# Rotated projections of a three-stage decoder layer: the cosine product moves to VectorE, the low part to GpSimd, and four PSUM banks take turns in all three projection phases

## The chip, the cores and the metric

The kernel runs on one core of a Trainium2 chip. The metric is the device time of one execution in microseconds (us): the median of three runs.

## The reference

Four sequences (batches) of 512 rows of width 512 go through three blocks, each with a residual. Below, LN is layer normalization without weights, RMS the root-mean-square one with weights.

```python
x = x + attn(LN(x))                    # 16 heads of 32, causal, no rotation
x = x + xattn(LN(x), ctx, pos, pos)    # 32 heads of 16, keys and values from ctx (width 256)
x = x + ffn(LN(x))                     # h = RMS(LN(x)); q, k, v = h @ w + b; 16 heads of 32, causal; then experts

# rotation of q and k in xattn: pairs of neighbouring elements
out = stack([x1 * cos - x2 * sin, x1 * sin + x2 * cos])
# rotation of q and k in ffn: halves of a head
q * cos + rot(q) * sin
```

## The kernel before

The program is a sequence of phases that are closed off from each other by a barrier of all engines: for each of the kinds `first`, `cross` and `rotary` a projection phase (line 244) and an attention core, and at the end the experts. The change lies in the projection phase. It makes q, k and v of all four batches and stores them in memory for the core. All products are made in three passes of high and low parts (`hi_lo_passes`), so each tensor that TensorE reads exists as a rounded high part and a remainder.

For each batch TensorE works through a ring of items: q, k and v of feature tile m = 0 to 3, in the order q0, k0, v0, q1, ... (in the last batch v2 and v3 come after k3). An item fills one PSUM bank with a 128x512 tile: q always takes 12 matmuls, k and v take 12 in `rotary` and 6 in `cross`, where the context is 256 wide. The ring has four banks (4 to 7), but only two (6 and 7) in `cross`, because the context's transposes sit in banks 4 and 5 (line 309). TensorE starts an item when the item N_RING places before it has been freed (`freed`, line 312). For q and k that is ScalarE's copy `straight`.

In what follows a **step** i is one q or k: i = 8 * batch + 2m, plus 1 for k, so there are 32. The rotation of step i goes over four engines:

- ScalarE copies the bank to `straight` (L538 with bias in `rotary`, L540 in `cross`), scaled for q.
- GpSimd multiplies `straight` by cosine into `turned` (L722).
- VectorE exchanges partitions of `straight` into `swapped` (L694, `stream_shuffle`), and GpSimd multiplies that by sine (L724).
- VectorE adds both (L645, `rotate`), ScalarE rounds the sum to its high part (L475, `high`), VectorE subtracts to get the low part (L650, `low`), and SyncE stores both (L384).

All these tiles have two slots. Every engine works in its own fixed order. VectorE does in step i: exchange i, low part i-2, sum i-1. ScalarE does: copy i, high part i-2. GpSimd does: cosine i, sine i, where cosine i waits for low part i-2, which frees its slot.

Beside that, the next batch's input is prepared in parts at fixed places (line 295). `NORM_AT = (0, 2, 4)` names the steps of a batch behind which VectorE does the parts of `norm`: statistics, centring (with sums of squares in `rotary`), and the second scaling in `rotary`. `ROOT_AT` names those behind which ScalarE takes the roots. `TURN_AT = 6` is the step behind which TensorE transposes the new input into banks 0 to 3 (`turn_in`, with the context behind it), ScalarE writes its high parts (`hT_high`) and VectorE its low parts (`hT_low`). TensorE's first q of the next batch waits for all of them.

In `rotary`, centring writes `h1`, which SyncE also stores to memory. There is one `h1` tile, so the centring of batch b+1 waits for the store of batch b (line 590), and that store stands in SyncE's queue behind all stores of batch b-1 (line 359 ff.). SyncE's queue also loads three stacks for the core in the middle of the last two batches (`STACK_AT`), ten transfers each in `cross` and five in `rotary`.

## Time and profile before

| | |
|---|---|
| median of 3 runs | 2296.25 us (2291.01 to 2301.59) |
| profiled execution: its own time | 2297.42 us |
| profiled execution: its span | 2295.6 us |
| mean granted clock of TensorE in it | 0.938 |
| TensorE busy | 2069.8 us (90%) |
| VectorE busy | 1237.3 us (54%) |
| ScalarE busy | 881.1 us (38%) |
| GpSimd busy | 708.3 us (31%) |
| first `straight` copy to last low part, `cross` | 472.9 to 615.4 us of the span |
| the same, `rotary` | 1081.9 to 1235.7 us |

The profile has one execution. Its time outside of the span is 1.8 us. The two projection phases that the change touches take together about 310 us of it. A page's row of a group gives busy time, count and mean; a row of a timeline gives the start in us, the duration in us, engine, line and operation, and in brackets the idle time before it with what ended it.

### The profile page before, as it was taken

What the parts mean: (1) busy time and instruction counts of PE and PEld (TensorE: products, weight loads), DVE (VectorE), ACT (ScalarE), POOL (GpSimd) and SP (SyncE); (2) the same over time, 40 slices, a digit from 0 to 9 for tenths busy, and PEclk for the clock granted to TensorE, in tenths of its full rate; (3) what the DMA queues carried; (4) which work ended last, traced back from release to release, by engine and by line L of the source; (5) the groups of instructions that cost most, each with busy time, mean ns of one, the idle gap of its engine ahead of it and who ended that gap; (6) DMA issues with size and microseconds to landing.
All of it is one profiled execution on the core that took longest, in us unless ns stands there. A gap on an engine that the chain in (4) does not pass through costs nothing. (4 is left out here: it accounts for less than half of the span.)

```text
span 2295.6 us, 31417 instructions
## 1 busy us (share of the span) xinstructions
PE 2069.8 (90%) x10679; PEld 1384.3 (60%) x10679; DVE 1237.3 (54%) x2679; ACT 881.1 (38%) x1662; POOL 708.3 (31%) x610
## 2 busy tenths in 40 slices
PE   6998999887689999996987999979999988999998
PEld 5775666565433434334776666657788877565664
DVE  5446656377689788875976656534313142222221
ACT  3335444343368676773334544433212210111111
POOL 0004555346513232322554654511000000233332
PEclk9997999989789999998997999889999998999999
DMA  5557666345654545443457665453012043433332
GB/s 188 172 192 174 140 136 136 113 163 217 254 127 100 132 116 152 103 124 117 179 192 227 151 152 128 102 200 110 30 63 74 1 172 117 142 60 59 63 65 36
DMA packets 149937, 297.14 MB, mean 129 GB/s; under 512 B 23762, under 2 KB 42324, under 8 KB 148756
## 3 DMA queue, kind: packets, MB, share of 16 engines
q1 hardware_dynamic: 113972, 243.73, 36.6%
q10 hardware_dynamic: 27072, 32.77, 5.3%
q0 software_dynamic: 8736, 18.62, 4.3%
q8 instruction: 88, 1.44, 0.3%
q14 instruction: 69, 0.57, 0.1%
HBM read 181.55 MB, written 102.50 MB: 124 GB/s over the span
## 5 line engine op out<-in xcount | busy, mean ns | idle before, releaser
L1157 ACT ACTIVATE cross_c_prob<-bank 128x512 f32<-128x512 f32 x512 | 271.3, 598 | 124.4 <-PE bank L996 123.4
L1194 DVE TENSOR_REDUCE cross_c_row_max<-bank 128x2 f32<-128x1024 f32 x256 | 300.0, 1212 | 34.8 <-PE bank L965 29.0
L996 PE MATMUL bank<-stack 56*128 56x512 f32 (+4 forms) x768 | 238.7, 437 | 34.1 <-DMA stack<-first_c_max_rows 11.4
L1577 PE MATMUL bank<-moe_hT,moe_w 128*128 128x512 f32 x1056 | 261.5, 405 | 2.2 <-DVE moe_hT L1819 2.2
L965 PE MATMUL bank<-stack 48*128 48x512 f32 (+4 forms) x768 | 218.1, 465 | 36.1 <-PEq L70 19.5
L1577 PEld LDWEIGHTS bank<-moe_hT,moe_w 128*128 128x128 f32 x1056 | 206.5, 197 | 47.3 <-DVE moe_hT L1819 2.6
L996 PEld LDWEIGHTS bank<-stack 56*128 56x128 f32 (+1 forms) x768 | 122.6, 198 | 164.8 <-ACT cross_c_prob L1157 70.3
L1665 PE MATMUL bank<-moe_w_e,moe_hT_e 128*128 x624 | 195.0, 466 | 1.6 <-DMA moe_w_e<-in_experts_packed 1.2
L965 PEld LDWEIGHTS bank<-stack 48*128 48x128 f32 (+1 forms) x768 | 107.4, 206 | 123.6 <-DVE cross_c_row_max L1194 51.7
L1190 DVE CUSTOM_DVE_ANT_0 first_c_masked<-bank,later 128x128 f32<-128x128 f32 (+3 forms) x256 | 115.8, 486 | 88.5 <-PE bank L965 87.6
L1190 DVE CUSTOM_DVE_ANT_0 rotary_c_masked<-bank,later 128x128 f32<-128x128 f32 (+3 forms) x256 | 116.0, 486 | 85.8 <-PE bank L965 84.9
L1157 ACT ACTIVATE rotary_c_prob<-bank 128x512 f32<-128x512 f32 (+3 forms) x256 | 105.5, 437 | 134.2 <-PE bank L999 132.7
L1157 ACT ACTIVATE first_c_prob<-bank 128x512 f32<-128x512 f32 (+3 forms) x256 | 105.2, 437 | 134.3 <-PE bank L999 133.0
L1665 PEld LDWEIGHTS bank<-moe_w_e,moe_hT_e 128*128 128x128 f32 x624 | 116.5, 192 | 63.5 <-issue 5.5
L1950 DVE TENSOR_TENSOR moe_prod<-moe_prod,bank 128x512 f32<-128x512 f32 x44 | 30.2, 687 | 205.7 <-PE bank L1577 205.7
L1037 PE MATMUL bank<-cross_c_prob,cross_c_v 128*32 128x512 f32 x1024 | 138.9, 615 | 0.6 <-DVE cross_c_flipped L1205 0.6
L1533 POOL DMA_INDIRECT out_x<-moe_res,moe_token x39 | 61.9, 1587 | 228.1 <-ACT moe_res L1774 228.1
L1588 PE MATMUL bank<-moe_w,moe_inner 128*128 128x512 f32 x528 | 127.9, 391 | 0.0
L999 PE MATMUL bank<-earlier_r,ident_r 128*128 128x128 f32 x512 | 125.7, 246 | 0.0
L1516 POOL TENSOR_TENSOR moe_res<-moe_res,moe_x_tile 128x512 f32<-128x512 f32 x16 | 23.3, 1455 | 323.1 <-DMA moe_x_tile<-x 323.1
L1588 PEld LDWEIGHTS bank<-moe_w,moe_inner 128*128 128x128 f32 x528 | 99.2, 188 | 21.5
L999 PEld LDWEIGHTS bank<-earlier_r,ident_r 128*128 128x128 f32 x512 | 105.5, 206 | 7.2
(344 smaller groups left out, 3967.8 us busy)
## 6 DMA issues: line engine op xcount, KB each, us to landing
moe_w_e<-in_experts_packed SPq DMA_DIRECT2D x8, 2176.0 KB, 9.0
qk_parts<-first_p_parts SPq DMA_DIRECT2D x32, 512.0 KB, 2.7
stack<-qk_parts SPq DMA_DIRECT2D x64, 256.0 KB, 6.9
qk_parts<-cross_p_parts SPq DMA_DIRECT2D x32, 512.0 KB, 2.7
stack<-qk_parts SPq DMA_DIRECT2D x256, 64.0 KB, 2.4
qk_parts<-rotary_p_parts SPq DMA_DIRECT2D x32, 512.0 KB, 2.7
moe_raw<-in_shared_packed SPq DMA_DIRECT2D x11, 768.0 KB, 11.5
stack<-qk_parts SPq DMA_DIRECT2D x16, 512.0 KB, 5.1
```

The source lines that it names most:

```text
L965: last = nc.tensor.matmul(bank[:, 0 : width_q(m)], q_stack[slot][r : r + PRODUCT_ROWS, at, m * P : (m + 1) * P], k_stack[slot][r : r + PRO ...
L996: last = nc.tensor.matmul(bank[:, 0 : S - q0], k_stack[slot][r : r + ALL_ROWS, at, m * P : (m + 1) * P], q_stack[slot][r : r + ALL_ROWS, a ...
L999: last = nc.tensor.matmul(bank[:, 0:P], c.ident_r[:], c.earlier_r[:], start=False, stop=True)
L1037: last = nc.tensor.matmul(psum[bank_o][32 * j : 32 * j + 32, q0:S], val, probability(g, m, j), start=m == 0, stop=m == TT - 1)
L1157: nc.scalar.activation(probability(g, step // HEADS_AT_ONCE, step % HEADS_AT_ONCE), psum[bank_at["score", n]][:, 0 : S - q0], ACT.Exp).the ...
L1190: nc.vector.tensor_tensor_reduce(out=masked[:, n % 2, 0 : width_q(m)], in0=bank[:, 0 : width_q(m)], in1=c.later[:, S - width_q(m) : S], sc ...
L1194: nc.vector.tensor_reduce(row_max[:, g % 2, m, j - 1 : j + 1], c.banks[:, first : first + WIDE, :], AX_X, ALU.max).then_inc(s.max_done, 1)
L1533: pool.indirect_dma_start(a.out, bass.IndirectOffsetOnAxis(ap=token[:, t : t + 1], axis=0), y[:, t % 2, :], None, bounds_check=B * S - 1, ...
L1577: last = nc.tensor.matmul(psum[bank][:], weights(pa, f, k), hT[p % 2][:, pb, k, :], start=m == 0, stop=m == len(steps) - 1)
L1588: last = nc.tensor.matmul(psum[SD[t]][:], inner[:, n % 2, pa, t * P : (t + 1) * P], w_d(pb, f), start=f == 0 and m == 0, stop=f == KF - 1 ...
L1665: last = nc.tensor.matmul(psum[1 + 2 * (t % 2) + half][:, 0:FE], hT_e[:, t % 2, k, :], rhs, start=k == 0, stop=k == KD - 1)
L1950: nc.vector.tensor_tensor(prod[:], prod[:], psum[SU][:], ALU.mult).then_inc(s.s_inner, 1)
```

## The change

`first` keeps its order; the rest holds for `cross` and `rotary`.

- VectorE makes the cosine product from the bank itself (`times_cos`, in `rotary` with the bias in the same instruction), in front of the exchange. The bank is now freed by that (`cos_made`) and no longer by ScalarE's copy. `turned` gets three slots.
- The low part goes from VectorE to GpSimd, behind the sine product of the following step; only the very last one stays on VectorE. ScalarE's high part moves one step forward: copy i is now followed by high part i-1 instead of i-2.
- The scale of q goes into the weights (`weights_high`, `weights_low`), so `straight` is an unscaled copy.
- The context is transposed into banks 0 and 1, behind step 5 (`CONTEXT_AT`), when the input's banks have been read; the ring has four banks in `cross` too. In batch 0 that happens behind q0.
- Norm parts move from behind steps 0, 2 and 4 to behind 0, 1 and 3, the roots from 2 and 4 to 1 and 3, the transposes from 6 to 4.

The diff, cut to its core:

```diff
+    TURNED_SLOTS = 3
-        NORM_AT, ROOT_AT, TURN_AT = (0, 2, 4), (2, 4), 6
+        NORM_AT, ROOT_AT, TURN_AT = ((0, 1, 3), (1, 3), 4) if rope else ((0, 2, 4), (2, 4), 6)
+        CONTEXT_AT = TURN_AT + 1
-        ring_banks = (6, 7) if cross else (4, 5, 6, 7)
+        ring_banks = (4, 5, 6, 7)
-            name = {...}.get(what, "straight_made" if rope else "parts_lo")
+            name = {...}.get(what, "cos_made" if rope else "parts_lo")
...
# TensorE
+                    def turn_context(bi):
+                        pe.wait_ge(s.ctx_loaded, 16 * (bi + 1))
+                        pe.wait_ge(s.hT_lo, t.n_in * bi + t.n_kv)
+                        for k in range(t.n_kv):
+                            for m in range(TT):
+                                last = nc.tensor.transpose(psum[k][:, m * P : (m + 1) * P], ctx_t[:, m, k * P : (k + 1) * P], c.ident[:])
+                        last.then_inc(s.transposed, 1)
...
+                        if cross and (bi, what, m) == (0, "k", 0):
+                            turn_context(0)
+                        if m == 0 and what in "qk":
+                            ready = t.n_in * bi + (KD if what == "q" else t.n_in)
+                            pe.wait_ge(s.hT_hi, ready)
+                            pe.wait_ge(s.hT_lo, ready)
...
+                        if cross and what in "qk" and 2 * m + (what == "k") == CONTEXT_AT and bi + 1 < BODY:
+                            turn_context(bi + 1)
...
# ScalarE
-                    hT_high(act, 0)
+                    hT_high(act, 0, range(KD))
                     weights_high(1)
+                    if cross:
+                        hT_high(act, 0, range(KD, t.n_in))
                     weights_high(2)
...
-                                act.wait_ge(s.cos_made, i - 1)
-                                nc.scalar.activation(straight[:, i % 2], bank[:], ACT.Copy, scale=scale).then_inc(s.straight_made, 1)
-                            if i >= 2:
-                                high(i - 2)
+                                nc.scalar.activation(straight[:, i % 2], bank[:], ACT.Copy).then_inc(s.straight_made, 1)
+                            if i >= 1:
+                                high(i - 1)
...
# VectorE
+                    def times_cos(i, what, m, bank):
+                        if i >= TURNED_SLOTS:
+                            dve.wait_ge(s.parts_hi, i - TURNED_SLOTS + 1)
+                            dve.wait_ge(s.parts_lo, i - TURNED_SLOTS + 1)
+                        dst, table = turned[:, i % TURNED_SLOTS], cos_t[:, i // n_qk if cross else 0]
+                        if rotary:
+                            nc.vector.scalar_tensor_tensor(dst, bank[:], bias_of(what, m), table, ALU.add, ALU.mult).then_inc(s.cos_made, 1)
+                        else:
+                            nc.vector.tensor_tensor(dst, bank[:], table, ALU.mult).then_inc(s.cos_made, 1)
...
                             dve.wait_ge(s.straight_made, i + 1)
+                            times_cos(i, what, m, bank)
                             nc.vector.stream_shuffle(swapped[:, i % 2], straight[:, i % 2], swap).then_inc(s.swap_made, 1)
-                            if i >= 2:
-                                low(i - 2)
                             if i >= 1:
                                 rotate(i - 1)
...
# GpSimd
-                            nc.gpsimd.tensor_tensor(turned[:, i % 2], straight[:, i % 2], cos_t[...], ALU.mult).then_inc(s.cos_made, 1)
                             pool.wait_ge(s.swap_made, i + 1)
                             nc.gpsimd.tensor_tensor(swapped[:, i % 2], swapped[:, i % 2], sin_t[...], ALU.mult).then_inc(s.sin_made, 1)
+                            if i >= 1:
+                                n = i - 1
+                                pool.wait_ge(s.parts_hi, n + 1)
+                                nc.gpsimd.tensor_tensor(parts[:, n % 2, 1], turned[:, n % TURNED_SLOTS], parts[:, n % 2, 0].bitcast(F32),
+                                                        ALU.subtract).then_inc(s.parts_lo, 1)
```

Two places show how rows move. The first is GpSimd's order in `cross`, two steps long (`axial_cos` and `axial_sin` are the tables, `parts` holds high and low part). Before:

```order
L722 TENSOR_TENSOR cross_p_turned<-cross_p_straight,axial_cos 128x512
L724 TENSOR_TENSOR cross_p_swapped<-cross_p_swapped,axial_sin 128x512
L722 TENSOR_TENSOR cross_p_turned<-cross_p_straight,axial_cos 128x512
L724 TENSOR_TENSOR cross_p_swapped<-cross_p_swapped,axial_sin 128x512
```

Now:

```order
L752 TENSOR_TENSOR cross_p_swapped<-cross_p_swapped,axial_sin 128x512
L756 TENSOR_TENSOR cross_p_parts<-cross_p_turned,cross_p_parts 128x512
L752 TENSOR_TENSOR cross_p_swapped<-cross_p_swapped,axial_sin 128x512
L756 TENSOR_TENSOR cross_p_parts<-cross_p_turned,cross_p_parts 128x512
```

The number of two-input products on GpSimd stays at two a step; the cosine product is gone and the low part of the step before stands behind the sine.

The second is VectorE's order in `rotary`, batch 0, around the scaling; `hn` is the scaled input of the next batch, `hT_lo` the low part of its transpose. Before: step 4, the scaling, step 5 and v2, with the low part of the transpose not before step 6 is done:

```order
L694 STREAM_SHUFFLE rotary_p_swapped<-rotary_p_straight 128x512
L650 TENSOR_TENSOR rotary_p_parts<-rotary_p_turned,rotary_p_parts 128x512
L645 TENSOR_TENSOR rotary_p_turned<-rotary_p_turned,rotary_p_swapped 128x512
L610 RECIPROCAL rotary_p_rstd<-rotary_p_rms 128x4
L612 TENSOR_SCALAR rotary_p_hn<-rotary_p_h1,rotary_p_rstd 128x512 x4
L694 STREAM_SHUFFLE rotary_p_swapped<-rotary_p_straight 128x512
L650 TENSOR_TENSOR rotary_p_parts<-rotary_p_turned,rotary_p_parts 128x512
L645 TENSOR_TENSOR rotary_p_turned<-rotary_p_turned,rotary_p_swapped 128x512
L683 TENSOR_TENSOR rotary_p_v<-bank,rotary_p_bv_row 128x512
```

Now, step 3, the scaling, v1, step 4 and the low part of the new input:

```order
L661 SCALAR_TENSOR_TENSOR rotary_p_turned<-bank,rotary_p_bias_raw,rotary_p_cos_t 128x512
L726 STREAM_SHUFFLE rotary_p_swapped<-rotary_p_straight 128x512
L670 TENSOR_TENSOR rotary_p_turned<-rotary_p_turned,rotary_p_swapped 128x512
L623 RECIPROCAL rotary_p_rstd<-rotary_p_rms 128x4
L625 TENSOR_SCALAR rotary_p_hn<-rotary_p_h1,rotary_p_rstd 128x512 x4
L714 TENSOR_TENSOR rotary_p_v<-bank,rotary_p_bv_row 128x512
L661 SCALAR_TENSOR_TENSOR rotary_p_turned<-bank,rotary_p_bias_q,rotary_p_cos_t 128x512
L726 STREAM_SHUFFLE rotary_p_swapped<-rotary_p_straight 128x512
L670 TENSOR_TENSOR rotary_p_turned<-rotary_p_turned,rotary_p_swapped 128x512
L466 SCALAR_TENSOR_TENSOR rotary_p_hT_lo<-bank,rotary_p_w_ln,rotary_p_hT_hi 128x512 x4
```

VectorE has three instructions a step in both; the low part's place is taken by the cosine product ahead of the exchange, and one step instead of two lies between the scaling and the low part of the transposed input.

## Rows read from the trace of the kernel before

**Rows 1.** By stretch: busy us of PE, PEld, DVE, ACT, POOL; PEclk, DMA, GB/s.

```profile
456.00:615.00 159.00, 116.16 (x480) 91.85 (x480) 114.54 (x208) 62.73 (x112) 95.70 (x64) 0.88 0.55 200
1060.00:1236.00 176.00, 146.55 (x640) 119.33 (x640) 141.97 (x275) 57.28 (x92) 93.40 (x64) 0.93 0.56 192
```

**Rows 2.** Waits in the cross phase: total us, times, longest us.

```profile
PE bank L434 <- DVE cross_p_hT_lo L457: 18.1, 4, 6.1
ACT cross_p_parts L475 <- DMA qk_parts<-cross_p_parts: 15.5, 4, 4.4
```

**Rows 3.** The same view of the rotary phase.

```profile
ACT rotary_p_straight L538 <- PE bank L434: 68.1, 24, 6.7
```

**Rows 4.** Timeline, rotary: two VectorE instructions (start us, duration us).

```profile
1126.82 0.68 DVE L683 TENSOR_TENSOR rotary_p_v<-bank,rotary_p_bv_row 128x512 f32<-128x512 f32 x1
...
1140.42 1.78 DVE L650 TENSOR_TENSOR rotary_p_parts<-rotary_p_turned,rotary_p_parts 128x512 fp32r<-128x512 f32 x1
```

**Rows 5.** Timeline of GpSimd in the same stretch.

```profile
1126.43 1.62 POOL L722 TENSOR_TENSOR rotary_p_turned<-rotary_p_straight,rotary_p_cos_t 128x512 f32<-128x512 f32 x1 [1.98 <-DVE rotary_p_parts L650]
...
1140.37 1.28 POOL L724 TENSOR_TENSOR rotary_p_swapped<-rotary_p_swapped,rotary_p_sin_t 128x512 f32<-128x512 f32 x1
```

**Rows 6.** Timeline of VectorE, last batch of the cross phase: two projections apart.

```profile
585.47 0.77 DVE L694 STREAM_SHUFFLE cross_p_swapped<-cross_p_straight 128x512 f32<-128x512 f32 x1
586.12 0.92 DVE L650 TENSOR_TENSOR cross_p_parts<-cross_p_turned,cross_p_parts 128x512 fp32r<-128x512 f32 x1
...
592.43 0.76 DVE L694 STREAM_SHUFFLE cross_p_swapped<-cross_p_straight 128x512 f32<-128x512 f32 x1
```

**Rows 7.** Timeline of ScalarE in the same stretch.

```profile
596.98 0.63 ACT L475 ACTIVATE cross_p_parts<-cross_p_turned 128x512 fp32r<-128x512 f32 x1 [2.13 <-DVE cross_p_turned L645]
597.52 0.58 ACT L540 ACTIVATE cross_p_straight<-bank 128x512 f32<-128x512 f32 x1
```

**Rows 8.** Timeline of ScalarE at the start of the cross phase.

```profile
466.78 1.10 ACT L487 ACTIVATE cross_p_w_hi<-raw 128x1024 fp32r<-128x1024 f32 x1
```

**Rows 9.** Tile swapped, cross: ns min/median/max, first and last start us.

```profile
L694 DVE STREAM_SHUFFLE cross_p_swapped<-cross_p_straight x32: 720/742/767, 473.5 to 607.2; 128x512 f32<-128x512 f32 x32
```

**Rows 10.** Tile parts, cross: the same columns.

```profile
L650 DVE TENSOR_TENSOR cross_p_parts<-cross_p_turned,cross_p_parts x32: 670/693/978, 479.8 to 614.7; 128x512 fp32r<-128x512 f32 x32
```

**Rows 11.** Tile parts, rotary: the same columns.

```profile
L650 DVE TENSOR_TENSOR rotary_p_parts<-rotary_p_turned,rotary_p_parts x32: 664/684/1798, 1091.3 to 1235.0; 128x512 fp32r<-128x512 f32 x32
```

**Rows 12.** Timeline of VectorE, rotary: first exchanges of batches 1 and 3.

```profile
1120.15 0.73 DVE L694 STREAM_SHUFFLE rotary_p_swapped<-rotary_p_straight 128x512 f32<-128x512 f32 x1
...
1201.80 0.73 DVE L694 STREAM_SHUFFLE rotary_p_swapped<-rotary_p_straight 128x512 f32<-128x512 f32 x1
```

**Rows 13.** Timeline of VectorE, rotary batch 1: norms and turned inputs of batch 2.

```profile
1121.97 2.46 DVE L576 BATCH_NORM_STATS2 rotary_p_stats<-xt 128x6 f32<-128x512 f32 x4
...
1132.72 1.91 DVE L592 TENSOR_SCALAR rotary_p_h<-xt,rotary_p_mv,rotary_p_rstd 128x512 f32<-128x512 f32 x4 [2.17 <-DMA h<-rotary_p_h]
...
1137.24 0.17 DVE L607 TENSOR_SCALAR rotary_p_ssq<-rotary_p_ssq 128x4 f32<-128x4 f32 x1
...
1142.93 3.52 DVE L612 TENSOR_SCALAR rotary_p_hn<-rotary_p_h,rotary_p_rstd 128x512 f32<-128x512 f32 x4
...
1151.76 2.71 DVE L455 SCALAR_TENSOR_TENSOR rotary_p_hT_lo<-bank,rotary_p_w_ln,rotary_p_hT_hi 128x512 fp32r<-128x512 f32 x4
```

**Rows 14.** Timeline of SyncE's queue, rotary.

```profile
1127.21 0.78 SPq L361 DMA_DIRECT2D h<-rotary_p_h  x1
```

**Rows 15.** Timeline of TensorE, rotary: the first matmul of batch 3.

```profile
1196.44 0.61 PE L434 MATMUL bank<-rotary_p_hT_hi,rotary_p_w_hi 128*128 128x512 f32 x1 [3.75 <-DVE rotary_p_hT_lo L455]
```

**Rows 16.** Timeline of ScalarE, rotary batch 3: copies of the first two projections.

```profile
1201.07 0.69 ACT L538 ACTIVATE rotary_p_straight<-bank,rotary_p_bias_q 128x512 f32<-128x512 f32 x1 [5.32 <-PE bank L434]
1203.81 0.69 ACT L538 ACTIVATE rotary_p_straight<-bank,rotary_p_bias_raw 128x512 f32<-128x512 f32 x1 [1.54 <-PE bank L434]
```

**Rows 17.** Busy time behind that idle time; 0.62 is PEclk.

```profile
1197.00:1201.00 4.00, 4.00 (x13) 3.14 (x12) 1.72 (x3) 0.00 (x0) 2.83 (x2) 0.62 0.64 224
```

More of the change, by code:

```diff
@@ L552, in _ @@
                             if i % n_qk == TURN_AT:
[L553 removed]
+                                hT_high(act, bi + 1, range(KD))
+                            if cross and i % n_qk == CONTEXT_AT:
+                                hT_high(act, bi + 1, range(KD, t.n_in))
                 @block.vector
@@ L706, in _ @@
                             if i % n_qk == TURN_AT:
-                                hT_low(dve, bi + 1)
+                                hT_low(dve, bi + 1, range(KD))
+                            if cross and i % n_qk == CONTEXT_AT:
+                                hT_low(dve, bi + 1, range(KD, t.n_in))
                 @block.gpsimd
```

63 lines of the change are left out of this document (28 added, 35 removed).

## The prediction

> **What bounds the kernel now.** I read the page first: TensorE is busy 90% of the span, but that is an average over seven phases, and the change touches two. So the next view is the busy time of these two stretches [rows 1]. In `cross`, 159 us long, TensorE works 116 us, VectorE 115 and GpSimd 96: nobody is full. In `rotary`, 176 us, TensorE has 147 and VectorE 142. The waits say who waits for whom. In `cross` TensorE stands 18.1 us in four places because the next input's low parts are late, and ScalarE waits 15.5 us for stores of `parts` to land [rows 2]. In `rotary` ScalarE waits 68.1 us for TensorE's banks [rows 3]: that phase goes at TensorE's pace.
>
> The timelines give the reason for the pace of `cross`. A VectorE subtraction with both inputs in SBUF took 1.78 us when a GpSimd product had started 0.05 us before it, and ended 0.55 us after that one [rows 4, 5]; undisturbed it takes 0.69 [rows 10]. They exclude each other. VectorE's addition with one input in a bank took 0.68 us right through a GpSimd product [rows 4, 5]. Before, each step holds two such VectorE instructions and two GpSimd products: 2 x 0.6 + 2 x 1.28 = 3.8 us where they all collide. Measured, two steps take 592.43 - 585.47 = 6.96 us, 3.48 a step [rows 6].
>
> **What the change does to a step.** It takes one of the excluded VectorE instructions away and puts a product with one input in a bank in its place. GpSimd keeps two products (2 x 1.28 [rows 5], plus 0.55 when it waits for the sum): 3.1 us. I price the cosine product at 0.68, by the addition out of a bank [rows 4]. The Trainium skill (Perfetto Trace Analysis, Optimizing Scalar/DVE Operations) gives VectorE an access overhead of about 125 ns on PSUM against 60 ns on SBUF; for 64 products that would be an estimated 4 us more. The row does not show it, 0.68 being no longer than the 0.69 of the subtraction in SBUF [rows 10], so my sum stays without it.
>
> But the change also ties a new knot. ScalarE's high part i-1 now stands in front of copy i+1, and it needs sum i-1, which VectorE makes last in step i. So the loop is: sum 0.68, signal 0.03, high part 0.54 until the next may start [rows 7], copy 0.58, signal 0.04, product 0.60, exchange 0.65 (the next instruction starts 0.65 after an exchange of 0.77 [rows 6]). That makes 3.1 us in `cross`, and 3.2 in `rotary`, whose copies take 0.69 [rows 16]. Before, high part i-2 left one step of slack there. So 3.48 becomes 3.1, but everything that VectorE does beside it now adds to the loop, less the 1.25 us in which ScalarE works. And where a v copy stands on ScalarE (`cross` only, about 0.5), it adds too.
>
> **The sum for `cross`.** Per batch: 8 x 3.1 = 24.8; statistics 3.1 (2.46 for the four [rows 13], 0.6 for the small ones) less 1.25 = 1.9; centring (1.9, plus 0.8 until high part and root are made, plus about 0.5 behind a GpSimd product) less 1.25 = 2.0; turned inputs 2.6 (four low parts behind ScalarE's four high parts); context and v2 1.7; v1 and v3 1.0. Together 34.0, three times; the first, with no sum to wait for, 33.4. The last batch has none of it: 7 x 3.1 + 2 x 0.5 = 22.7. The stack loads in SyncE's queue hold two stores up by some 3.4 us each; a wait of 4.4 is in the trace [rows 2], and ScalarE now stands in the loop while it waits: 6.8. First to last exchange: 33.4 + 68.0 + 22.7 + 6.8 = 130.9, before 607.2 - 473.5 = 133.7 [rows 9]. The start is later by 3.1: the context's copies and the third weight split (1.1 on ScalarE [rows 8]) now stand between q0 and its copy, and the product is ahead of the exchange. The end is earlier by 2.3: the last low part came 8.1 us behind the last exchange [rows 9, 10]; now exchange 0.74, sine 1.3, a low part in front 1.3, sum, high and low 2.0, waits 0.5, which is 5.8. Sum: -2.8 + 3.1 - 2.3 = **-2.0 us**.
>
> **The sum for `rotary`.** One projection is 2.74 us of TensorE [rows 16], twelve a batch 32.8, so a batch can't take less than 35 with its transposes. Before, two batches took 1201.80 - 1120.15 = 81.65 us [rows 12]. Now TensorE transposes behind q2 (step 4) and needs the scaling behind step 3. It gets there early and loses its lead: at best it is three items ahead. I walk from the end of that scaling: last transposes 0.5; k2, v2, q3, k3, v3, q0 6 x 2.74 = 16.4; copy 0.7; step 0 1.95; statistics 3.1; step 1 1.95. Then centring waits for the `h1` store. That store was issued 0.9 us behind low part 7 and landed 5.5 us later (1127.21 [rows 14] to 1132.72 [rows 13], a wait of 2.17); now low part 7 is GpSimd's, behind the sine of step 0, and ends 4.3 us after the copy, so `h1` lands at 10.8, and VectorE, ready at 7.8, stands 3.0 us. Centring and squares 4.7 (1132.72 to 1137.41 [rows 13]), v0 0.7, step 2 1.95, step 3 with the loop 3.25, root 0.8, scaling 2.7 (between 1.9 free and 3.52 beside GpSimd [rows 13]). From the copy on that is 24.9; a batch takes 17.6 + 24.9 = 42.5. Two: 85.0, which is +3.4. In batch 0 TensorE stands about 6 us for the scaling, half of which the vanished wait at the batch's end (3.75 in one case [rows 15]) gives back: +3.2. In the last batch the eleven items behind q0 give 30.1 us from its first exchange to the end, against 1235.7 - 1201.8 = 33.9 [rows 11, 12]: -3.7. Then the clock: behind 3.75 us of idle time [rows 15] the granted clock was 0.62 (between the levels of 1.2 and 2.4 GHz) [rows 17], and q0 took 1201.07 - 1196.44 = 4.6 us instead of 2.74 [rows 15, 16], 1.9 lost. TensorE will now stand some 4 to 6 us at three transposes; I count two of three: +3.8. Sum: **+6.7 us**.
>
> Nothing else moves: the scale in the weights costs nothing, as the same copy takes it along, and its cover is the same wait for the inputs. The profiled execution's own time is 2297.4 us, 1.2 above the median of the runs. 2297.4 - 2.0 + 6.7 = 2302.1, less 1.2: **2301 us**. A measurement of this kernel can tell about 0.5% (11.5 us) from no change, so the forecast is: no difference.
>
> **Rivals.**
>
> *Faster: the side work hides.* My terms beside the loop (9.2 us a batch in `cross`) add fully. VectorE's own busy time is only 115/4 = 28.6 us a batch [rows 1]; if four banks let it run through without gaps, three batches save 34.0 - 28.6 = 5.4 each (16), and if the stores also keep up, 6.8. With TensorE never waiting at the transposes `rotary` ends at its pace, some 5 us before today instead of 6.7 after (12). 2301 - 16 - 7 - 12 = 2266 at the far end, half way 2283. For it: 18.1 us of waits at the batch's end vanish [rows 2]. Against it: the order on ScalarE is fixed. Chance 0.2.
>
> *Slower: TensorE loses its lead and its clock.* Besides the transposes it must wait for the bank of v0, which VectorE frees only behind centring and squares; that is 3 us idle in front of q2. If each of those six gaps is followed by a slow projection, 1.9 each, `rotary` gains 7.6 us on top, and each wait for `h1` may be 3 us longer where the store lands late: 2301 + 7.6 + 6 = 2315. It decides from gaps of about 3.75 us on [rows 15], the shortest after which these rows show a slow projection. Chance 0.2.
>
> *Slower: stores.* `parts` has two slots, and high part i waits for the store of i-2. I leave about 1 us of slack a step. If stores take 1.5 us more, each second step pays: 32 x 0.75 = 24, so 2325. The 15.5 us of such waits [rows 2] speak for it, the steadier order against it. Chance 0.07.
>
> *The change doesn't free the engines.* If the product out of the bank excludes GpSimd too, up to 1.1 us (1.78 - 0.68) is lost on it, on half of 64 products 35 us: 2336. Rows 4 and 5 speak against it. Chance 0.03.
>
> **Numbers.** Forecast 0.5, faster 0.2, slower 0.2 + 0.07 + 0.03. Faster by over 0.5% (below 2284.8) takes 0.18 of the faster case and 0.02 of the forecast's own spread: 0.2. Slower (above 2307.7) takes 0.17, 0.07 and 0.03 of the three and 0.02 of the forecast: 0.29. Within: 0.51. The range leaves out the far ends on both sides: 2280 to 2318.
>
> **What would show it.** In the profile after: exchanges in `cross` 3.1 to 3.6 us apart in the last batch, against 3.48; no VectorE subtraction of 1.8 us but sums of up to 1.9; the products out of the bank at 0.68 beside GpSimd; no wait of TensorE for low parts at the batch's end, but in `rotary` one of 3 to 6 us in front of the transposes; centring waiting about 3 us for `h1`; first exchanges of `rotary` batches 1 and 3 near 1121 and 1210 (moved with the end of `cross`). Wrong: exchanges under 3.0 us apart, or `rotary` batches under 38 us, would make it faster; products of 1.2 us and more, or waits of ScalarE for stores above 30 us in a phase, slower.

## The result, and the profile after

| | before | changed |
|---|---|---|
| median of the runs beside the prediction (4 each) | 2297.61 us (2291.01 to 2301.59) | 2319.79 us (2318.73 to 2322.35) |
| ratio, 95% interval | | 1.0101 (1.0075 to 1.0127) |
| timed again on one chip (23 and 6 runs) | 2301.03 us | 2322.79 us, 1.0099 (1.0080 to 1.0118) |
| profiled execution: own time, span | 2297.42, 2295.6 us | 2320.35, 2318.5 us |

Slower by 1.0%, the interval clear of no change: forecast 2301 (2280 to 2318), measured 2320. Below, "first to last exchange" is the pace of a phase; "front" is from the phase's first statistics instruction to its first exchange, "tail" from the last exchange's start to the start of the last low part. They are read from the tile views.

| us | before | changed | forecast change | measured change |
|---|---|---|---|---|
| cross: front | 19.8 | 21.7 | +3.1 | +1.9 |
| cross: first to last exchange | 133.7 | 139.0 | -2.8 | +5.3 |
| cross: tail | 7.5 | 4.9 | -2.3 | -2.6 |
| rotary: front, exchanges, tail together | 175.8 | 187.4 | +6.7 | +11.6 |
| all other stretches | 1958.8 | 1965.5 | 0 | +6.7 |

The exchanges of both phases, changed kernel, tile view (ns min/median/max, first and last start in us), against 473.5 to 607.2 before [rows 9]:

```profile
L726 DVE STREAM_SHUFFLE cross_p_swapped<-cross_p_straight x32: 715/730/754, 480.3 to 619.3; 128x512 f32<-128x512 f32 x32
...
L726 DVE STREAM_SHUFFLE rotary_p_swapped<-rotary_p_straight x32: 715/732/754, 1092.2 to 1249.8; 128x512 f32<-128x512 f32 x32
```

Busy time by stretch, changed kernel (columns as in [rows 1]; the stretches are chosen alike):

```profile
461.00:624.00 163.00, 111.70 (x480) 89.93 (x480) 102.10 (x208) 60.69 (x111) 90.47 (x63) 0.86 0.54 194
1070.00:1255.00 185.00, 150.61 (x640) 123.30 (x640) 130.58 (x273) 56.71 (x92) 91.56 (x63) 0.91 0.52 178
```

VectorE did lose work: 114.5 us busy in cross became 102.1, 142.0 in rotary 130.6 [rows 1]. Yet both phases got longer, and every engine stands more. The waits say for what. Changed kernel, cross, then rotary (total us, times, longest us):

```profile
ACT cross_p_parts L486 <- DVE cross_p_turned L670: 66.5, 27, 5.1
POOL cross_p_swapped L752 <- DVE cross_p_swapped L726: 65.2, 32, 21.9
DVE cross_p_turned L663 <- ACT cross_p_straight L551: 38.1, 22, 4.7
...
PE bank L407 <- DVE cross_p_hT_lo L468: 23.1, 3, 7.7
ACT cross_p_parts L486 <- DMA qk_parts<-cross_p_parts: 21.0, 5, 5.4
...
ACT rotary_p_parts L486 <- DVE rotary_p_turned L670: 98.0, 30, 10.0
...
DVE rotary_p_turned L661 <- ACT rotary_p_straight L549: 33.2, 19, 5.1
...
PE bank L443 <- DVE rotary_p_v L714: 8.5, 3, 3.5
```

ScalarE waits for VectorE's sum (L670), and VectorE for ScalarE's copy (L551): each for the other, in turn. In rotary ScalarE waited 68.1 us for TensorE before [rows 3]; now it waits 98.0 for the sum. The phase no longer goes at TensorE's pace.

### The profile page after: what moved, and what is told of

Read it like the earlier page. It is cut to its first block, busy times and chain, and to the rows that moved or that the text cites. A ratio compares the mean times of both kernels' runs of the same rounds, so it can differ in the third digit from the quotient of the medians.

```text
span 2318.5 us, 31374 instructions
## 1 busy us (share of the span) xinstructions
PE 2073.8 (89%) x10679; PEld 1387.6 (60%) x10679; DVE 1218.2 (53%) x2681; ACT 878.8 (38%) x1662; POOL 700.8 (30%) x608
## 4 chain that ended last, share of the span: by engine, by line
PE 52%; DVE 12%; DMA 5%; issue 5%; ACT 2%; POOL 1%; SPq 1%; ACTq 0%; POOLq 0%; DVEq 0%
PE bank L1610 10%; PE bank L1698 8%; PE bank L1070 4%; PE bank L1621 4%; PE bank L1717 4%; PE bank L443 4%; PE bank L998 4%; PE bank L1029 4%; DVE cross_c_row_max L1227 4%; PE bank L1087 3%; DMA stack<-rotary_c_max_rows 1%; DMA stack<-cross_c_max_rows 1%; DMA normed<-xt 1%; PE bank L1038 1%; PE bank L1032 1%
## 5 line engine op out<-in xcount | busy, mean ns | idle before, releaser
L1070 PE MATMUL bank<-cross_c_prob,cross_c_v 128*32 128x512 f32 x1024 | 139.0, 615 | 0.6 <-DVE cross_c_flipped L1238 0.6
L1032 PE MATMUL bank<-earlier_r,ident_r 128*128 128x128 f32 x512 | 125.9, 246 | 0.0
```

What stands on the lines that cost most here:

```text
L1032: last = nc.tensor.matmul(bank[:, 0:P], c.ident_r[:], c.earlier_r[:], start=False, stop=True)
L1070: last = nc.tensor.matmul(psum[bank_o][32 * j : 32 * j + 32, q0:S], val, probability(g, m, j), start=m == 0, stop=m == TT - 1)
```

## The loop and the context, read from the trace

The step itself is what I had forecast. Changed kernel, VectorE in the last steps of cross batch 1 (start us, duration us, then the idle time before and its releaser):

```profile
538.93 0.73 DVE L726 STREAM_SHUFFLE cross_p_swapped<-cross_p_straight 128x512 f32<-128x512 f32 x1
539.55 0.68 DVE L670 TENSOR_TENSOR cross_p_turned<-cross_p_turned,cross_p_swapped 128x512 f32<-128x512 f32 x1
541.97 1.29 DVE L468 TENSOR_TENSOR cross_p_hT_lo<-bank,cross_p_hT_hi 128x512 fp32r<-128x512 f32 x2 [1.74 <-ACT cross_p_hT_hi L459]
545.67 0.69 DVE L663 TENSOR_TENSOR cross_p_turned<-bank,axial_cos 128x512 f32<-128x512 f32 x1 [2.42 <-ACT cross_p_straight L551]
...
546.29 0.74 DVE L726 STREAM_SHUFFLE cross_p_swapped<-cross_p_straight 128x512 f32<-128x512 f32 x1
546.92 0.68 DVE L670 TENSOR_TENSOR cross_p_turned<-cross_p_turned,cross_p_swapped 128x512 f32<-128x512 f32 x1
548.78 0.69 DVE L663 TENSOR_TENSOR cross_p_turned<-bank,axial_cos 128x512 f32<-128x512 f32 x1 [1.19 <-ACT cross_p_straight L551]
...
549.39 0.74 DVE L726 STREAM_SHUFFLE cross_p_swapped<-cross_p_straight 128x512 f32<-128x512 f32 x1
```

From exchange 546.29 to 549.39 is a plain step: 3.10 us. The sum ends its part, ScalarE makes high part and copy, and VectorE stands 1.19 us before the product. The step before it, 538.93 to 546.29, is the one with the context: 7.36 us, 4.26 more than a plain one, where I had allowed 1.7. TensorE and ScalarE show why (same columns):

```profile
537.36 1.94 PE L407 MATMUL bank<-ident,cross_p_ctx_t 128*128 128x128 f32 x8 [7.70 <-DVE cross_p_hT_lo L468]
```

```profile
540.82 0.63 ACT L486 ACTIVATE cross_p_parts<-cross_p_turned 128x512 fp32r<-128x512 f32 x1 [2.98 <-DMA qk_parts<-cross_p_parts]
541.35 1.06 ACT L459 ACTIVATE cross_p_hT_hi<-bank 128x512 fp32r<-128x512 f32 x2
542.31 0.60 ACT L533 ACTIVATE cross_p_v<-bank 128x512 f32<-128x512 f32 x1
545.04 0.60 ACT L551 ACTIVATE cross_p_straight<-bank 128x512 f32<-128x512 f32 x1 [2.14 <-PE bank L443]
```

The context goes into the inputs' banks, so TensorE can't start it before VectorE has made the inputs' low parts out of them. It stands 7.70 us, holds back every projection queued behind, and ScalarE then waits 2.14 us for the next bank. Three times that, 23.1 us. Before, TensorE waited for low parts too, 18.1 us in front of the first items of the four batches [rows 2]; but of those only 3.3 us are left when the places of the side work move and nothing else (below, "The kernel before, new places in cross alone"). The 23.1 us come with turning the context apart.

## Experiments

Ratios are against the kernel before on the same chip; the lengths of phases are from each run's profile.

**The kernel before, again.** No edit.

> The kernel before, unchanged, profiled once more. The changed kernel's profile is 22.9 us longer than the one of before, of which some 16 lie in the two projection phases and 4.2 + 3.9 in code that the change does not touch (the first core phase and what follows the second rotary core). If these two are spread between executions, this run shows stretches of untouched code that differ by 2 to 4 us from the first profile of before, while cross (133.7 from first to last exchange) and rotary (145.8) stay within 1 us. If the change costs them too (by what it leaves behind in queues), both stay as they were within 1 us.

Span 2304.2 us, 8.6 over the first profile. Cross 134.0, rotary 145.7: both within 0.3 us. From the last low part of the first projection to the cross statistics 296.5 instead of 291.2; from the experts' first VectorE product (L1950) to the end 753.5 instead of 748.0. So the untouched code is what varies; the projections can be compared to a few tenths here. Over all pairs of profiles with the same code in a phase their lengths agree within 1.4 us. Over all 18 profiles the untouched stretches add up to between 1957 and 1973 us.

**High part i-2 in the changed kernel.**

```diff
-                            if i >= 1:
-                                high(i - 1)
+                            if i >= 2:
+                                high(i - 2)
...
-                                n = i - 1
+                            for n in ([i - 2] if i >= 2 else []) + ([i - 1] if i == BODY * n_qk - 1 else []):
```

> High part i-2 instead of i-1 behind copy i, low part on GpSimd likewise; everything else as changed. Theory A (the loop sum, high part, copy, product, exchange through ScalarE makes all side work additive): the loop is cut, the last cross batch goes at GpSimd's pace (about 3.0 a step instead of 3.1), steps with statistics and centring get shorter by up to 1.2 us each; cross first to last exchange 139.0 becomes 131 to 134, rotary 157.6 becomes 150 to 153, the ends grow by 1 to 2 us each; whole kernel 8 to 13 us faster than the changed one. Theory B (the early places of scaling and transposes cost TensorE its lead, the loop is beside the point): both stretches move by less than 3 us, whole kernel within 4 us of the changed one.

2354.05 us, ratio 1.0209 (1.0179 to 1.0240); cross 147.5, rotary 178.5. Neither theory had this. Plain steps are 4.41 us apart, and the row says why (VectorE, last cross batch):

```profile
607.85 0.69 DVE L663 TENSOR_TENSOR cross_p_turned<-bank,axial_cos 128x512 f32<-128x512 f32 x1 [2.51 <-POOL cross_p_parts L755]
```

The product now waits for GpSimd's low part. With three slots I had opened one loop and closed another, so this run says nothing on the first.

**The old places for the side work.** One line; centring, roots and transposes as before, in both phases.

```diff
-        NORM_AT, ROOT_AT, TURN_AT = ((0, 1, 3), (1, 3), 4) if rope else ((0, 2, 4), (2, 4), 6)
+        NORM_AT, ROOT_AT, TURN_AT = (0, 2, 4), (2, 4), 6
```

> Centring, roots and turned inputs back at the steps where they stood before (0, 2, 4; 2, 4; 6), the context one step behind; everything else as changed. Theory B: rotary's TensorE waits for low parts and scaling get shorter by 2 to 3 us in three batches and its clock stays up, rotary first to last exchange 157.6 becomes 147 to 150; the wait for the store of h1 (2.93 each, twice) vanishes, since centring of the second batch's part stands a step later; whole kernel 6 to 10 us faster. Theory A: the sum of VectorE's work in the loop is the same, only its place differs; rotary gains at most the 5.9 us of the two waits for h1, cross nothing.

2307.75 us, ratio 1.0007 (0.9989 to 1.0026). Rotary 157.6 became 146.9, cross 139.0 became 136.6. TensorE's clock in rotary, first to last exchange (columns as in [rows 1]), changed kernel and this run:

```profile
1092.20:1249.80 157.60, 139.17 (x598) 113.98 (x597) 109.05 (x234) 45.13 (x79) 88.26 (x61) 0.95 0.50 174
```

```profile
1093.30:1240.20 146.90, 135.56 (x594) 110.26 (x593) 111.33 (x235) 45.06 (x79) 88.14 (x61) 0.97 0.54 187
```

TensorE is busy 3.6 us less for the same matmuls (some 1 us of it are four matmuls that this trace lacks), at a higher clock, and idle for 11.3 us instead of 18.4. Theory B is borne out in place, and in rotary all but in size (146.9 against 147 to 150). The whole was not as expected: the ratios of this kernel and the changed one lie 0.9% apart, some 22 us, where the two phases give 13.

**The store of `h1` earlier.** In SyncE's queue the store of the next batch's `h1` stands ahead of that of k2.

> The store of h1 of the next batch goes into SyncE's queue ahead of that of k2 instead of behind the batch's last store. The wait of VectorE for it (2.93, twice, in rotary) should vanish. Theory A: VectorE is in the loop, so the whole 5.9 us come off rotary's 157.6. Theory B: TensorE's stands set the pace of rotary, and centring is only one link before them: 3 to 6 us. If neither (the wait is covered by others): less than 2 us. In cross nothing changes.

2323.48 us, ratio 1.0081 (1.0055 to 1.0107). The wait is gone, and rotary is 153.5 instead of 157.6: 4.1 us, as Theory B had it. The whole time doesn't show it; this run's untouched stretches are the longest of all, 1973 us. The phase answers, the total does not.

**Transposes at 6, centring early.**

```diff
-        NORM_AT, ROOT_AT, TURN_AT = ((0, 1, 3), (1, 3), 4) if rope else ((0, 2, 4), (2, 4), 6)
+        NORM_AT, ROOT_AT, TURN_AT = ((0, 1, 3), (1, 3), 6) if rope else ((0, 2, 4), (2, 4), 6)
```

> Centring and roots stay at the changed kernel's early steps (0, 1, 3; 1, 3), only the transposes go back from step 4 to 6. Theory B1 (it is the place of the transposes that costs rotary its 10.7 us, since at step 4 TensorE reaches them before the scaling is done, and all twelve items until the next ones start late): rotary, first to last exchange, 157.6 becomes 146 to 149; cross near the 136.6 of the run with all old places. Theory B2 (it is the early centring, with VectorE's stand for the store of h1): rotary stays at 154 to 158, since that stand remains.

2323.02 us, ratio 1.0101 (1.0075 to 1.0127). Rotary 153.6: between the two theories. The transposes' place gives 4.0 of the 10.7 us, the place of centring, scaling and roots the other 6.7, and VectorE still stands 6.1 us for the store of `h1`, as it does in the changed kernel (6.0). In cross, 146.3, both missed: ScalarE waits up to 6.3 us for a store in the step before the transposes of the inputs. Why that store is later here was not tried.

**The kernel before with the new places.**

```diff
-        NORM_AT, ROOT_AT, TURN_AT = (0, 2, 4), (2, 4), 6
+        NORM_AT, ROOT_AT, TURN_AT = ((0, 1, 3), (1, 3), 4) if rope else ((0, 2, 4), (2, 4), 6)
```

> The kernel before (cosine product on GpSimd, low part on VectorE, high part i-2, context turned with the inputs, two banks in cross) with the new places alone (0, 1, 3; 1, 3; 4). If the places cost rotary its time whatever the step loop is, rotary becomes 155 to 160 instead of 145.7, as in the changed kernel. If the places only cost because VectorE stands in the new loop, it stays within 3 us of 145.7. Cross: the transposes for inputs and context at step 4 meet low parts that are done at once; 130 to 137 against 133.8.

2304.18 us, ratio 1.0015 (0.9999 to 1.0030). Rotary 160.9, a little above my 155 to 160: TensorE waits there 10.2 us for the bank of v0 and 9.6 us for the scaled input, and centring 11.5 us for the store of `h1`. **Cross 122.2**: 11.5 us shorter than before and below my range. That one line is worth more in cross than I had forecast for the whole change, and rotary takes it back.

**Cross new with the context at 6, rotary old.**

> Rotary with the old places, cross with the new ones (4), but the context's transposes at step 6 instead of 5. If the 7.35 us from exchange 5 to exchange 6 in cross come from TensorE waiting for the inputs' low parts before it may reuse their banks (7.7 us), that step falls to about 4.5 and cross from 139.0 to 131 to 134 in three batches; rotary is 146 to 148 as in the run with all old places. Whole kernel: 3 to 6 us under the run with all old places. If the context costs the same wherever it stands, cross stays at 137 to 140.

2301.73 us, ratio 1.0006 (0.9992 to 1.0021). Cross 133.4, rotary 145.5. The step from exchange 5 to 6 of batch 1 fell from 7.36 to 4.36 us (531.76 to 536.12), as expected. But the context now stands in the next step, which rose from 3.10 to 4.29, so the move gives 1.8 us in this batch. Cross came where it should, rotary 0.5 us below. The whole missed: level with before, its ratio the same as that of the run with all old places, not 3 to 6 us under it.

**High part i-2, exchange ahead of the product, old places.**

> The first run with high part i-2 closed another loop that I had not seen: the product for i waits for GpSimd's low part i-3, which stands behind sine i-1, and exchange and sine i stand behind the product (0.69 + 0.74 + 1.29 + 1.29 + signals = 4.4 a step, 4.41 measured). Here the exchange goes ahead of the product, so that loop opens; places as before. Theory A (the loop through ScalarE makes side work additive): steps beside statistics and centring up to 1.2 us shorter than in the run with all old places, plain steps 3.0 to 3.1; cross 136.6 becomes 130 to 133, rotary 146.9 becomes 141 to 145. Theory B: plain steps as fast, but both stretches within 2 us of 136.6 and 146.9, because TensorE's waits at the transposes set the batch.

2326.05 us, ratio 1.0102 (1.0077 to 1.0127); cross 139.1, rotary 157.4. Both theories missed. Plain steps did fall, in the last cross batch to 2.8 to 3.2 us (exchanges at 592.72, 595.51, 598.48, 601.54, 604.72), but another wait took over, here in its cross phase:

```profile
ACT cross_p_parts L486 <- DMA qk_parts<-cross_p_parts: 42.2, 14, 6.9
```

A low part made by GpSimd a step later leaves a step later for memory, and `parts` has two slots.

**Low part back on VectorE, high part i-2 and i-1.** GpSimd keeps the sine product alone; the product out of the bank stays on VectorE. `cross` has the new places, `rotary` the old ones. The two kernels differ only in this, and in the lines that go with it at the end of the last batch:

```diff
-                            if i >= 2:
-                                high(i - 2)
+                            if i >= 1:
+                                high(i - 1)
```

> Cosine product stays on VectorE, the low part goes back to VectorE (i-2), high part i-2; GpSimd has the sine product alone. Cross with the new places and the context at step 5, rotary with the old places. VectorE then has 0.69 + 0.65 + 0.67 + 0.68 = 2.7 a step, excluded pairs 0.67 + 0.68 + 1.28 = 2.6. Theory C (GpSimd's late low part delays the store, and ScalarE waits for the slot: 42.2 us in 14 waits in the run with high part i-2 and the exchange first): those waits fall to under 15 us in cross, plain steps to 2.7 to 2.9, cross 139.0 to 115 to 125, rotary to 138 to 145, whole kernel 10 to 20 us faster than before. If the low part on GpSimd is not what costs, cross stays above 132.

> The same with high part i-1 in front of copy i+1, as the change has it: the only difference to the run before it. Theory A (sum, high part, copy, product, exchange form a loop through ScalarE, 3.1 us, beside which side work adds fully): plain steps 3.1, cross 8 to 15 us longer than in the run before it, rotary 3 to 8 longer. Without such a loop: within 2 us of it in both.

2328.47 us, ratio 1.0119 (1.0086 to 1.0153), and 2386.97 us, ratio 1.0371 (1.0340 to 1.0403). Cross 140.7 and 172.0, rotary 161.8 and 184.1. Theory C missed: the waits for stores are down to 8.2 us, yet plain steps take 3.52. The sums of the first of the two (ns min/median/max):

```profile
L663 DVE TENSOR_TENSOR cross_p_turned<-bank,axial_cos x32: 675/678/692, 479.8 to 620.5; 128x512 f32<-128x512 f32 x32
L670 DVE TENSOR_TENSOR cross_p_turned<-cross_p_turned,cross_p_swapped x32: 677/1768/1785, 485.2 to 624.0; 128x512 f32<-128x512 f32 x32
```

The sum, both inputs in SBUF, meets the sine product in most steps and takes 1.77 us instead of 0.68; the product out of the bank is never stretched. Of the second kernel Theory A had the loop right and the size far too small (8 to 15 us in cross and 3 to 8 in rotary; measured 31.3 and 22.3): with high part i-1 the slow sum lies in the loop. From its start to that of the high part are 1.79 us, then to copy, product, exchange, low part and next sum 0.54, 0.61, 0.62, 0.61 and 0.59, together 4.76; plain exchanges are 4.79 apart (635.29, 640.08). One `high` moved by a step costs 31 us in cross. The plain step alone, 1.27 us longer, would make 39 in 31 steps, so what costs here is the step and not side work that adds. And high part i-2 alone doesn't let a loop catch up: in the first kernel batch 1 takes 38.7 us against 28.2 for eight plain steps, 10.5 us of side work. VectorE works there without a gap in a plain step.

**The kernel before, new places in cross alone.**

```diff
-        NORM_AT, ROOT_AT, TURN_AT = (0, 2, 4), (2, 4), 6
+        NORM_AT, ROOT_AT, TURN_AT = ((0, 1, 3), (1, 3), 4) if cross else ((0, 2, 4), (2, 4), 6)
```

> The kernel before with the new places in cross alone; rotary keeps the old ones. The two profiles at hand give the parts: cross 122.2 with the new places and the old step loop, rotary 145.8 with the old places. If the two phases are independent, cross is 122 to 124, rotary 145 to 147, and the whole kernel 10 to 12 us faster than before (ratio 0.995). If the gain in cross is given back behind it (the core that follows waits for something else), cross is as short but the whole within 4 us of before.

**2288.23 us, ratio 0.9946 (0.9927 to 0.9964)**: a little faster than before, and so than the changed kernel. Cross 121.8, rotary 144.9. TensorE's waits for low parts in cross, 18.1 us before [rows 2], are down to the first one:

```profile
PE bank L434 <- DVE cross_p_hT_lo L457: 3.3, 1, 3.3
```

How the old loop takes the side work, VectorE, cross batch 1:

```profile
511.54 0.72 DVE L694 STREAM_SHUFFLE cross_p_swapped<-cross_p_straight 128x512 f32<-128x512 f32 x1
...
513.57 3.65 DVE L592 TENSOR_SCALAR cross_p_hn<-xt,cross_p_mv,cross_p_rstd 128x512 f32<-128x512 f32 x4
...
517.15 0.73 DVE L694 STREAM_SHUFFLE cross_p_swapped<-cross_p_straight 128x512 f32<-128x512 f32 x1
...
519.18 0.75 DVE L694 STREAM_SHUFFLE cross_p_swapped<-cross_p_straight 128x512 f32<-128x512 f32 x1
...
522.38 1.33 DVE L645 TENSOR_TENSOR cross_p_turned<-cross_p_turned,cross_p_swapped 128x512 f32<-128x512 f32 x1 [1.63 <-POOL cross_p_swapped L724]
...
523.84 0.74 DVE L694 STREAM_SHUFFLE cross_p_swapped<-cross_p_straight 128x512 f32<-128x512 f32 x1
```

A step with centring, 5.61 us, is followed by one of 2.03, together 7.64. Steps of this loop go in such pairs without side work too, in the last batch 2.31 and 4.65, together 6.96; so centring costs 0.7 us here. In the changed kernel its step takes 5.88, 2.8 more than a plain one, and no step is under 3.09. By batch: batch 1 takes 33.4 us here against 27.4 for eight steps at the last batch's mean of 3.43, which leaves 6.0 for the side work; in the changed kernel 36.9 against 24.8, which leaves 12.1. The shorter plain step saves 2.6 us a batch, and the side work beside it costs 6.1 more.

**The same, and transposes of rotary at 5.**

> As the run before it, and in rotary the transposes one step earlier, at 5 instead of 6, centring unmoved. Theory B (TensorE reaches the transposes before the scaling is done, when they stand early): scaling is done behind step 4, TensorE is two to three items ahead, so it stands there 2 to 4 us but no longer 3.1 us for low parts at the batch's end: rotary 144 to 152. Step 4 gave 160.9, step 6 gave 145.8; a value near 160 would mean that any step before 6 is too early.

2305.10 us, ratio 1.0008 (0.9992 to 1.0025). Rotary 155.5, above my 144 to 152: one step too early already costs 10 us; of the steps 4, 5 and 6 only 6 holds. Which wait makes it 155.5 was not looked at.

**Banks and context apart, old loop.** The changed kernel with the cosine product back on GpSimd, the low part on VectorE and high part i-2, the bank freed by ScalarE's copy and two slots of `turned`; the scale stays in the weights; cross new, rotary old; context at step 5, then 6.

> The change without its step loop: four banks in cross and the context turned apart in the inputs' banks at step 5, but the cosine product on GpSimd, the low part on VectorE, high part i-2 as before; cross with the new places, rotary with the old. If the step loop is what costs cross its 17 us, cross is 118 to 126 (two banks more can only let TensorE run ahead). If the context turned apart is what costs (TensorE waits 7.7 us for low parts at each of three), cross is 134 to 139. In between, both.

> The same with the context's transposes at step 6 instead of 5. In the changed step loop that move gave 5.6 us (139.0 to 133.4). If the wait of TensorE for the inputs' low parts costs the same beside the old loop, cross is 4 to 7 us under that of the run with step 5; if the old loop hides it, within 2 us.

2297.07 us, ratio 0.9980 (0.9966 to 0.9995), and 2294.35 us, ratio 0.9974 (0.9959 to 0.9990). Cross 125.9 and 123.7: the first at the upper end of my 118 to 126, where the step loop is what costs cross its 17 us. TensorE stands 19.0 us for the low parts there, nearly as long as in the changed kernel (23.1), and the phase is 3.7 us over the one without that stand. Moving the context gives 2.2 us here, not the 5.6 of the changed loop. Rotary, 145.5, is as before (145.8), with the scale in the weights.

**The changed kernel and the best one, again.** No edit against those two.

> The changed kernel itself, unchanged, timed in more rounds. If the 1.010 was right: 1.008 to 1.012 against the kernel before on the same chip. If before's first four runs were low by the spread of untouched code (its later medians were 2300.9 to 2304.6, in place of 2297.6): about 1.007, some 17 us. The stretches of the two projections stay within 1 us of the first profile (139.0 and 157.6), the untouched first core and the part behind the second core vary by up to 6 us.

> The kernel before with the new places in cross alone, timed again beside the changed kernel on one chip. The first measurement gave 0.9946, with the interval 0.9927 to 0.9964: again 0.993 to 0.996, and 25 to 32 us under the changed kernel. Its cross 121 to 123, rotary 144 to 147.

2322.79 us, ratio 1.0099 (1.0080 to 1.0118); cross 139.3, rotary 157.0. And 2290.71 us, ratio 0.9952 (0.9933 to 0.9970); cross 122.7, rotary 146.1. The 1.010 was right, and the two kernels are 32 us apart on one chip.

**The ledger that closes.** First to last exchange, us, adding one part of the change at a time:

| | cross | rotary |
|---|---|---|
| before | 133.7 | 145.8 |
| + new places | 122.2 (-11.5) | 160.9 (+15.1) |
| + four banks, context apart at step 5 | 125.9 (+3.7) | (not run with new places) |
| + step loop: the whole change | 139.0 (+13.1) | 157.6 (-3.3) |

The row of the banks holds the scale in the weights as well, and was run with cross alone at the new places; cross with and without rotary's new places is 122.2 and 121.8. In rotary the change of banks touches nothing, and the loop is worth -3.3 at the new places, +1.1 at the old ones (146.9 against 145.8; the run with the context at 6 has the same code in rotary and 145.5, so this is no more than the spread). The loop's +13.1 in cross is by batch (the run with the context at 5, "banks5", against the changed kernel, first exchange to first exchange): 30.4 and 35.8, 36.1 and 36.9, 35.1 and 37.3, last 24.3 and 29.1. The last one has no side work. In both kernels ScalarE waits for stores there, twice each; banks5, then the changed kernel:

```profile
ACT cross_p_parts L486 <- DMA qk_parts<-cross_p_parts: 7.3, 2, 3.7
```

```profile
ACT cross_p_parts L486 <- DMA qk_parts<-cross_p_parts: 10.4, 2, 5.4
```

Only in the changed loop do steps show it, 6.60 and 6.48 us long; in banks5 none of that batch is over 4.65.

No run takes high part i-1 alone out of the changed loop: the two that tried closed another wait. So the +13.1 is shown for the loop as a whole, and its share of lag and of order is not.

## Why the prediction was wrong

The forecast for the profiled execution was 2302.1 us; it took 2320.4, 18.2 more: 6.6 in cross, 4.9 in rotary, 6.7 elsewhere. The step that failed most is the term "context and v2" of the sum for cross; in rotary it is the last batch, where I had put a wait for a store at nothing.

- **The step of 3.1 us: right.** 3.10 in cross, 3.25 in rotary, and 3.57 with a v copy. The product out of the bank took 0.69 in cross (678/691/695 ns; 0.75 in rotary, with the bias) and didn't mind GpSimd: the one at 532.84 ran 0.69 us inside a GpSimd low part (532.26, 1.26 us). That rival (0.03) fell. The Trainium skill (Perfetto Trace Analysis, Optimizing Scalar/DVE Operations) would have had it dearer than one in SBUF. The trace has, with both inputs in SBUF, the last low part at 692 ns and the sums at a median of 675; so of the 65 ns between the page's two figures at most 16 show.
- **The sum of cross per batch: 34.0 forecast, 36.9 measured** (batch 1). By terms: statistics 1.75 for 1.9; centring, with the copy of v0, 2.8 for 2.0; turned inputs 2.4 for 2.6; v1 and v3 0.97 for 1.0; context and v2 **4.26 for 1.7**. Over the three batches that term is 12.5 us for 5.1, 7.4 of the 8.1 by which first to last exchange missed. The failed step is "context and v2 1.7": I priced copies and low parts, and not that TensorE must wait for the banks of the inputs before the context's transposes, up to 7.7 us in each of three batches. The run with the context at 6 bears it out: those waits for low parts fall from 23.1 to 9.1 us and cross by 5.6.
- **Last batch of cross: right**, 29.1 for 29.5. **Front and tail**: +1.9 for +3.1, -2.6 for -2.3.
- **Rotary: mechanism right, one term missing.** Centring waited 2.93 us for `h1` (forecast 3.0), and TensorE 3.38 for v0's bank (3 in the slower rival); these rows of the changed kernel:

```profile
1144.14 1.92 DVE L605 TENSOR_SCALAR rotary_p_h<-xt,rotary_p_mv,rotary_p_rstd 128x512 f32<-128x512 f32 x4 [2.93 <-DMA h<-rotary_p_h]
```

```profile
1149.50 0.50 PE L443 MATMUL bank<-rotary_p_hT_hi,rotary_p_w_hi 128*128 128x512 f32 x1 [3.38 <-DVE rotary_p_v L714]
```

  The batches are 44.25 and 44.4 us for 42.5: the two took 88.7, where 81.65 [rows 12] + 3.4 + 3.8 for the clock makes 88.9. Batch 0 took 41.75 against 37.3, +4.5 for +3.2, and the front, for which I had no change, took 0.8 more. In front of the transposes TensorE stood 2.10 and 0.68 us in batch 1, not the 4 to 6 that I had counted the clock by; the clock fell behind the stand for v0's bank as well. So of the 88.7 the walk is borne out, and that the clock's 3.8 fits is partly luck. The first exchanges of batches 1 and 3 came at 1133.96 and 1222.62, both some 13 us later than my 1121 and 1210, so the lengths between them agree. The term that failed is the last batch, forecast at 3.7 us less than before; from its first exchange to the start of the last low part it took 32.5 us against 33.2, 0.7 less. The row that I had no term for:

```profile
1231.62 0.63 ACT L486 ACTIVATE rotary_p_parts<-rotary_p_turned 128x512 fp32r<-128x512 f32 x1 [6.46 <-DMA qk_parts<-rotary_p_parts]
```

  One step takes 7.67 us (1225.87 to 1233.54), 4.4 more than a plain one, because ScalarE stands in the loop until a store has landed. Before, the same batch had such a wait of 1.0 us. I had counted these waits in cross (6.8) and not here. My point of decision for the clock, gaps of 3.75 us and more, was also too high (last section).
- **"Nothing else moves": open.** 6.7 of the profile's 22.9 us lie in untouched code, well inside its spread of 16. But the medians of 23 and 6 runs on one chip are 21.8 us apart, and the two phases explain about 16. The other 5 to 6 were not traced to a place; they stay open.
- **The rivals.** The nearest number is that of the slower one on TensorE's lead (2315, chance 0.2). Its wait for v0's bank came, and a lower clock behind it (last section), but not its price: batches 1 and 2 of rotary took what the forecast had, not 7.6 us more. Its number is near because cross and the last batch of rotary added what it didn't have; that is luck. The faster rival said that the side work hides; in the old loop with the new places half of it does, in the new one it doesn't.
- **What the sum didn't ask.** I set the new loop's plain step (3.1) against the old one's (3.48) and let the side work add to the new, without asking what the old loop does with side work at better places. With the new places alone the old loop keeps its mean plain step of 3.43 us, of which GpSimd works 2.9 (20.3 us in seven steps), and takes a batch's side work for 6.0 us more, where the new loop pays 12.1. Of cross before, 11.5 us lay in the places. So the change mended the wrong limit.

## What to carry to other kernels

Split a change into its one-line parts and run each alone: here the moved places were worth -11.5 us in one phase and +15.1 in the other, and kept where they help they beat both kernels (0.9946). A faster plain step is no gain if it takes the slack out of a loop: compare whole batches with their side work. In the changed loop the side work of batch 1 costs 12.1 us, in the old one at the same places 6.0. A lag of two steps is not enough for that: the loop with the low part back on VectorE has it, and adds 10.5 us in batch 1. And where a buffer is used twice in turn, price the engine's stand for its release, with all that is queued behind it.

## What the runs showed of the hardware

- An instruction of VectorE with both inputs in SBUF next to a GpSimd product: 1.77 us (median of 32 sums) instead of 0.68, where the order made them meet in most steps. GpSimd pays as well: its sine product is 1.63 us in the changed kernel (1632 ns median), where the sum stands in its way, and 1.29 with the exchange first, where then GpSimd's low part pays (1736 ns) and the sum too (1404 ns). In the pairs looked at, it is the one that starts later: in the changed kernel the sum at 530.49 took 0.68 and the sine product at 530.67 took 1.62.
- A product with one input in a bank: 0.68 to 0.69 us (medians) in cross in all versions, never over 0.70, beside GpSimd or not.
- The granted clock fell after shorter stands than the 3.75 us that I had taken from the trace of before. Changed kernel, rotary batch 1 (columns as in [rows 1]): full clock; 0.65 behind the stand of 3.38 us at 1149.50, and 0.62 behind the one of 2.10 us at 1156.20, 7 us later, both between the levels of 1.2 and 2.4 GHz; nearly full again from 1160 on. Batch 2 repeats it: 0.69 behind a stand of 3.54 us, 0.57 behind one of 2.10. The last row is cross behind the stand of 7.70 us.

```profile
1134.00:1149.00 15.00, 12.12 (x54) 9.71 (x52) 11.07 (x31) 2.51 (x5) 5.79 (x4) 1.00 0.47 182
...
1149.00:1153.00 4.00, 3.50 (x10) 2.74 (x11) 2.73 (x6) 1.21 (x2) 2.17 (x2) 0.65 0.00 0
...
1156.00:1160.00 4.00, 3.12 (x17) 2.91 (x17) 4.00 (x8) 0.00 (x0) 1.18 (x1) 0.62 0.90 265
1160.00:1165.00 5.00, 5.00 (x23) 4.20 (x22) 3.72 (x7) 3.52 (x6) 2.90 (x2) 0.96 0.61 234
...
537.00:546.00 9.00, 8.64 (x32) 7.29 (x33) 4.84 (x10) 3.52 (x7) 2.99 (x3) 0.69 0.75 291
```
